# A fused attention and expert kernel on one core: slot product from PSUM, rows loaded in quarters, setup and weight work in another order

## The chip, the cores and the metric

The kernel runs on one core of a Trainium2 chip. A core has five engines that run side by side: TensorE (PE in the profile; its weight loads are PEld), VectorE (DVE), ScalarE (ACT), GpSimd (POOL) and SyncE (SP), and 16 DMA engines that move data between HBM and the on-chip memory SBUF. PSUM is the memory that TensorE writes. The metric is the device time in microseconds (us) of one execution.

## The reference, cut to what matters

```
x: 32 batches x 256 tokens x 128; 16 heads of 8; 8 experts, top 2, hidden 256
mod = silu(c) @ wmod -> shift, scale, gate for both halves (sa, ca, ga, sb, cb, gb)
h = layernorm(x) * (1 + ca) + sa
q, k, v = h @ w_qkv.T + b_qkv;  std = q.k / sqrt(8)
write_lines, read_lines = exterior products of four 4-vectors per head, each over its norm
incidence = read_lines . J(write_lines)
logits = std + incidence * decay ** (distance) * bias_scale  for the past;  causal mask
x = x + ga * (softmax(logits) @ v @ w_out.T + b_out)
h = layernorm(x) * (1 + cb) + sb
the two largest of h @ Wg take the token; out = sum of weight * (silu(h@W1) * (h@W2)) @ W3
x = x + gb * out
```

## The kernel before

It has three parts, each a block with one program per engine. Between two blocks all engines meet.

**setup** loads the weights and x, turns the projection matrices, works out the modulation `mod`, the decay table `decay` (16 heads x 128 distances per partition) and many constants. SyncE loads the projection weights, x in eight parts (L232) and then the experts' W1, W2 (L235) and W3 (L236). GpSimd makes masks and clears tiles, stores zero rows to HBM with four DMAs of its own queue (L286), and last of all cuts the decay table by an affine select (L295), after ScalarE's exponential (L345). VectorE fills the decay's arguments (L395) and only then takes the modulation and its gates (L398 to L408).

**attend** runs a pipeline written out by hand. An iteration b = -4 ... 35 has eight slots p = 0 ... 7, and each slot works for several batches at once: on batch b the scores and exponentials of heads 2p and 2p+1, on batch b+1 the prescores (a bound on the maximum of each row), on b+2 and b+3 the projections and the lines, on b-1 the output, on b-2 the second norm and the routing, on b-3 the ranks and the scatter to the experts' rows. The table JOBS says in which slot TensorE does which small job. Every engine runs its list in order and waits on semaphores.

Per slot TensorE does `scores` (L631 to L633) into the one tile sc, `incidences` (L620) and `prescores` (L644 to L646) into the one tile pre. VectorE adds tt to sc (L794), makes the next tt out of inc and decay (L827) and takes the maxima of pre (L806, and L811 after four of them). ScalarE takes the exponential (L1033). 

The keys and queries go through HBM: they are split in three bf16 parts (high, middle, low) and stored by SyncE (L554), six DMAs for the dims and twelve for the lines of a batch, and read back as rows with three DMAs per half of the heads (L579 KT 480 KB, L580 queries 336 KB, L581 QI 144 KB). TensorE waits for a half in front of its first prescores, in slots 1 and 5 of iteration b for batch b+1. In SyncE's list a half of rows follows the load of peaks (L586), which waits for ScalarE, and is followed by the next stores. GpSimd works out the low part of the lines (L1133) in slot 3, behind the outer products (L1236, four instructions) and the crosses (L1245, L1247: one and three instructions) of slot 2; in slot 4 the counts (L1208, L1210) and the first scatter follow.

Routing on VectorE, slot 3, for batch b-3: L820 adds the experts' bases to the ranks that TensorE left in PSUM (L738 to L741), L880 multiplies by the choice `hot`, L885 takes the maximum, which is the row to scatter to, and L889 to L894 work out the two weights. GpSimd scatters with four indirect DMAs (L1223).

After the last iteration ScalarE copies the experts' weights into w_hi (L1112) and VectorE, behind the table of tiles (L950 to L970), subtracts to get w_lo (L974).

**experts** runs 136 tiles of 128 rows over a ring of 16: SyncE loads a tile (L1358), TensorE turns and multiplies it (L1377 to L1402). ScalarE's first instruction is the load of the gate rows (L1439, 2 MB, first read at the very end).

## Time and profile before

| | us |
|---|---|
| median of three timed runs | 1242.65 |
| lowest, highest | 1239.29, 1244.85 |
| the profiled execution | 1247.23 |
| its span in the trace | 1245.4 |
| TensorE busy (share of the span) | 996.9 (80%) |
| VectorE busy | 909.1 (73%) |
| ScalarE busy | 716.2 (58%) |
| GpSimd busy | 815.0 (65%) |
| DMA queue of SyncE, share of 16 engines | 43.3% |

The shares are averages over three very different stages: setup up to 28.8 us, attention up to about 940, experts and the final sum after that. The rows further down come from five views. Busy time by stretch gives for a stretch of the span what each engine worked. The timeline gives instructions in order: start, duration, engine, line, operation, output and inputs, count, and in brackets the engine's idle time in front of it with what ended it. Groups by line give the count, busy time and mean of all instructions of a line within a stretch, and the idle time in front of them. Waits give who waited for whom. The DMA issues give size and time to landing.

### The profile page before, as it was taken

How to read it: one execution, taken by the hardware profiler on the slowest of the kernel's cores; microseconds unless marked ns; L12 is line 12 of the kernel's file. 1: busy time of each engine (PE TensorE's matmuls, PEld its weight loads, DVE VectorE, ACT ScalarE, POOL GpSimd, SP SyncE). 2: the span in 40 equal slices, each digit the busy share in tenths (PEclk: the TensorE clock that was granted, in tenths of full speed). 3: DMA queues.
4: the chain of work that ended last, by engine and by line, in shares of the span. 5: the costliest groups of instructions: out<-in, count | busy, mean ns of one | idle time of the engine just before them, and what ended most of it. 6: DMA issues, size and time to landing. Idle time of an engine off the chain costs nothing. (4 is left out here: it accounts for less than half of the span.)

```text
span 1245.4 us, 30939 instructions
## 1 busy us (share of the span) xinstructions
PE 996.9 (80%) x9409; PEld 783.2 (63%) x9409; DVE 909.1 (73%) x2318; ACT 716.2 (58%) x1612; POOL 815.0 (65%) x1381
## 2 busy tenths in 40 slices
PE   2348888989898989998898989887725888888767
PEld 2236667766677767776777767766524777777653
DVE  6347888878898899889988998888644454444437
ACT  3326676767767776767776777764433444444430
POOL 6676667877787878787787878773351555555440
PEclk9999999999999999999999999999956999999988
DMA  9056565565656565656656565654113222222229
GB/s 284 29 147 161 135 163 146 157 163 133 178 139 176 142 174 146 169 149 163 158 150 167 154 165 142 176 136 130 35 43 118 77 69 73 73 74 76 67 83 352
DMA packets 206097, 170.44 MB, mean 137 GB/s; under 512 B 56944, under 2 KB 183408, under 8 KB 205808
## 3 DMA queue, kind: packets, MB, share of 16 engines
q1 hardware_dynamic: 194400, 143.21, 43.3%
q0 software_dynamic: 8704, 18.04, 4.7%
q10 hardware_dynamic: 2832, 7.20, 1.5%
q8 instruction: 81, 1.33, 0.5%
q14 instruction: 80, 0.66, 0.2%
HBM read 90.81 MB, written 76.78 MB: 135 GB/s over the span
## 5 line engine op out<-in xcount | busy, mean ns | idle before, releaser
L1033 ACT ACTIVATE PT<-sc 128x768 f32<-128x768 f32 x256 | 206.7, 807 | 234.7 <-DVE sc L794 224.8
L806 DVE TENSOR_REDUCE peak<-pre 128x6 f32<-128x768 f32 x256 | 243.6, 952 | 88.4 <-PE pre L646 82.3
L1542 POOL DMA_INDIRECT yab<-y_out,xt x136 | 131.4, 966 | 143.3 <-DVE y_out L1488 106.8
L794 DVE TENSOR_TENSOR sc<-sc,tt 128x512 f32<-128x512 f32 x256 | 176.8, 691 | 17.2 <-PE sc L633 16.1
L1223 POOL DMA_INDIRECT xg<-stage,slot_i x128 | 130.6, 1020 | 76.8 <-DVE stage L894 46.0
L827 DVE TENSOR_TENSOR tt<-inc,decay 128x512 f32<-128x512 f32 x256 | 174.2, 681 | 0.3 <-PE inc L620 0.3
L631 PE MATMUL sc<-queries,KT 128*128 128x256 bf16 x512 | 142.1, 278 | 34.5 <-ACT PT L1033 24.9
L644 PE MATMUL pre<-KT,queries 120*128 120x128 bf16 x512 | 115.7, 226 | 58.3 <-DMA QI<-kq_rows 52.8
L646 PE MATMUL pre<-causal,identb 128*128 128x256 bf16 x512 | 143.2, 280 | 0.0
L645 PE MATMUL pre<-KT,queries 120*128 120x256 bf16 x512 | 141.9, 277 | 0.0
L633 PE MATMUL sc<-identb,causal 128*128 128x256 bf16 x512 | 140.7, 275 | 0.0
L1452 ACT ACTIVATE silu<-up 128x256 f32<-128x256 f32 x136 | 52.8, 388 | 127.8 <-PE up L1386 109.2
L1495 DVE TENSOR_TENSOR hid<-silu,up 128x256 f32<-128x256 f32 x136 | 57.0, 419 | 81.0 <-ACT silu L1452 51.0
L632 PE MATMUL sc<-queries,KT 128*128 128x128 bf16 x512 | 112.9, 220 | 0.0
L644 PEld LDWEIGHTS pre<-KT,queries 120*128 120x128 bf16 x512 | 50.9, 99 | 86.6 <-DMA QI<-kq_rows 62.1
L631 PEld LDWEIGHTS sc<-queries,KT 128*128 128x128 bf16 x512 | 51.0, 100 | 77.7 <-ACT PT L1033 61.7
L620 PE MATMUL inc<-QI,KT 128*128 128x128 bf16 x1024 | 99.7, 220 | 0.1
L1236 POOL TENSOR_TENSOR outer<-lines 128x256 f32<-128x256 f32 x128 | 89.1, 726 | 5.7 <-ACT lines L997 5.7
L1402 PE MATMUL y<-w,hidT 128*128 x544 | 86.9, 284 | 2.6 <-ACT hidT L1462 1.3
L660 PE MATMUL pv<-PT,VP 128*32 128x256 f32 x1024 | 84.1, 391 | 1.5 <-ACT PT L1033 1.5
L1488 DVE TENSOR_SCALAR y_out<-y,xt 128x128 f32<-128x128 f32 x136 | 47.2, 347 | 50.1 <-PE y L1402 43.6
L1394 PE MATMUL hidT_ps<-ident,hid 128*128 128x128 f32 x272 | 55.4, 287 | 32.6 <-DVE hid L1495 30.9
(263 smaller groups left out, 2824.1 us busy)
## 6 DMA issues: line engine op xcount, KB each, us to landing
KT<-kq_rows SPq DMA_DIRECT2D x64, 480.0 KB
queries<-kq_rows SPq DMA_DIRECT2D x64, 336.0 KB
kq_rows<-dim_part SPq DMA_DIRECT2D x64, 192.0 KB, 3.0
kq_rows<-line_part SPq DMA_DIRECT2D x64, 144.0 KB
QI<-kq_rows SPq DMA_DIRECT2D x64, 144.0 KB
xt<-xg SPq DMA_DIRECT2D x136, 65.0 KB
kq_rows<-dim_part SPq DMA_DIRECT2D x64, 128.0 KB, 2.8
kq_rows<-line_part SPq DMA_DIRECT2D x64, 96.0 KB
```

Source lines behind the costliest of these rows:

```text
L631: nc.tensor.matmul(sc[:, n, 0:T], KT[par][:, h, 0:P], QF[par][:, h, :], start=True, stop=False)
L632: nc.tensor.matmul(sc[:, n, T:3 * P], KT[par][:, h, P:T], QF[par][:, h, P:T], start=False, stop=False)
L633: last = nc.tensor.matmul(diagonal(sc, n), causal[:], identb[:].unsqueeze(1).broadcast_to([P, 2, P]), start=False, stop=True)
L644: nc.tensor.matmul(pre[:, n, 0:P], QF[par][0:TOP, h, 0:P], KT[par][0:TOP, h, 0:P], start=True, stop=False)
L645: nc.tensor.matmul(pre[:, n, P:3 * P], QF[par][0:TOP, h, P:T], KT[par][0:TOP, h, :], start=False, stop=False)
L646: last = nc.tensor.matmul(diagonal(pre, n), identb[:], causal[:].unsqueeze(1).broadcast_to([P, 2, P]), start=False, stop=True)
L794: nc.vector.tensor_tensor(diag, diag, tt[p % 2][:], ALU.add).then_inc(added.sem, 1)
L806: nc.vector.reduce_max(peak[half][:, i:i + 2, 0:3], pre[:, :, 0:3 * P].rearrange("p n (g k) -> p n g k", g=3), AX.X)\
L827: nc.vector.tensor_tensor(tt[p % 2][:], inc[:], decay[:, 2 * p:2 * p + 2, :].unsqueeze(2).broadcast_to([P, 2, NT, P]), ALU.mult).then_inc( ...
L1033: nc.scalar.activation(PT[p % 4][:], sc[:, :, 0:3 * P], ACT.Exp).then_inc(exped.sem, 1)
L1223: nc.gpsimd.indirect_dma_start(xg[0:E * CAP, :], bass.IndirectOffsetOnAxis(slot_i[:, t, k:k + 1], 0), stage[par][:, t, k, :], None).then_i ...
L1542: nc.gpsimd.indirect_dma_start(yab, bass.IndirectOffsetOnAxis(xt[r][:, D:D + 1].bitcast(i32), 0), y_out[r % 8][:], None).then_inc(y_sent[r ...
```

## The change

What it does, in the order of the diff:

(In the diff a long run of removed lines, and unchanged lines, are cut to "...", and eight columns of indentation are left out.)

- setup: the loads of W1, W2 and W3 go from SyncE's setup list to the head of its attention list. The four DMAs of zero rows go from GpSimd to ScalarE, which waits for their landing at the end of setup. TensorE's modulation products go ahead of the bias columns, VectorE's modulation and gates ahead of the decay's arguments, and the store of the gate rows ahead of the decay's exponential. The decay's mask goes into attention, to GpSimd's slot 7 of iteration -4; VectorE waits for it before its first use.
- rows: each half is loaded as two quarters of four heads, six DMAs where there were three, with a semaphore per quarter, and TensorE waits in every second slot.
- rank: TensorE adds the experts' bases itself with a product of the identity and `ebase`; VectorE then needs one product from PSUM, in place of a sum from PSUM and a product in SBUF.
- GpSimd: the crosses are parted from the outer products and go behind the lines' low part.
- the experts' weights: a copy per slot on ScalarE in iteration 32, a subtraction per slot on VectorE in iteration 33.
- experts: the load of the gate rows goes to tile 16.

```diff
@@ -230,10 +231,6 @@
             sp.dma_start(v["x_all"][:, n * k * D:(n + 1) * k * D].rearrange("p (n d) -> p n d", d=D), xd[:, n * k:(n + 1) * k, :]).then_inc(ld_x, 16)
-        w_raw = v["w_lo"][:].bitcast(fp32).rearrange("p e (n h) -> p e n h", n=2)
-        for n, w in enumerate(("W1", "W2")):
-            sp.dma_start(w_raw[:, :, n, :], v[w].rearrange("e p h -> p e h")).then_inc(v["w_loaded"], 16)
-        sp.dma_start(v["w3"][:], v["W3"].rearrange("e (m p) d -> p e m d", p=P)).then_inc(v["w_loaded"], 16)
         sp.wait_ge(ld_x, 128)
@@ -279,22 +276,13 @@
         step(nc.gpsimd.tensor_copy(v["identb"][:], ident[:]))
-        step(nc.gpsimd.memset(zero_rows[:], 0.0))
-        for par in range(2):
...
+        nc.gpsimd.memset(zero_rows[:], 0.0).then_inc(zeros_ok, 1)
         ones_pair = 0x3F803F80
...
             step(nc.gpsimd.memset(v["VP"][m][:, :, :, DH:DH + 1], 1.0))
-        pool.wait_ge(exp_ok, 1)
-        nc.gpsimd.affine_select(out=decay[:], in_=decay[:], compare_op=ALU.is_gt, fill=0.0, base=0,
-                                pattern=[[0, H], [1, P]], channel_multiplier=-1).then_inc(setup_done, 1)
-        pool.wait_ge(setup_done, 1)
@@ -308,21 +296,21 @@
         last.then_inc(wT_ok, 1)
+        pe.wait_ge(silu_ok, 1)
+        for m in range(6):
+            last = nc.tensor.matmul(tC[:, m * NB:(m + 1) * NB], wmod_sb[:, m * D:(m + 1) * D], silu_c[:],
+                                    start=True, stop=True)
+        last.then_inc(mod_ok, 1)
         pe.wait_ge(az_ok, 2)
...
                          start=True, stop=True).then_inc(columns_ok, 1)
+        pe.wait_ge(gates_ok, 1)
+        nc.tensor.transpose(tA[0:NB, 0:D], mod[:, 5, :], ident[:]).then_inc(rows_ok, 1)
         pe.wait_ge(columns_ok, 2)
         nc.tensor.matmul(tD[:, 4:5], v["w_outT"][:], bias_v[:], start=True, stop=True).then_inc(out_bias_ok, 1)
-        pe.wait_ge(silu_ok, 1)
-        for m in range(6):
...
@@ -340,15 +328,23 @@
         nc.scalar.activation(lz[:], ez[:], ACT.Ln, bias=1.0).then_inc(ln_ok, 1)
-        act.wait_ge(arg_ok, 1)
-        nc.scalar.activation(v["line_decay"][:], v["line_decay"][:], ACT.Exp, scale=line_log[:]).then_inc(act_step, 1)
-        nc.scalar.activation(decay[:], decay[:], ACT.Exp).then_inc(exp_ok, 1)
+        act.wait_ge(zeros_ok, 1)
+        for par in range(2):
+            for kq, half in ((0, 1), (1, 0)):
+                main = v["kq_rows"][par][kq, 0:RAW0].rearrange("(s r) h t -> r h s t", s=NS)[DH:NM]
+                act.dma_start(main.rearrange("r h s t -> (r h) s t")[:, :, half * P:half * P + P],
+                              zero_rows[0:6 * H].unsqueeze(1).broadcast_to([6 * H, NS, P])).then_inc(v["zeros_stored"], 16)
         act.wait_ge(ld_v, 64)
         act.wait_ge(rows_ok, 1)
-        nc.scalar.activation(v["modr"][:], tA[0:NB, 0:D], ACT.Copy)\
-          .then_inc(act_step, 1)
-        act.wait_ge(act_step, 3)
+        nc.scalar.activation(v["modr"][:], tA[0:NB, 0:D], ACT.Copy).then_inc(act_step, 1)
+        act.wait_ge(act_step, 2)
         act.dma_start(v["mod_rows"], v["modr"][:]).then_inc(v["mod_stored"], 16)
+        act.wait_ge(columns_ok, 2)
+        nc.scalar.activation(v["line_decay"][:], v["line_decay"][:], ACT.Exp, scale=line_log[:])
+        act.wait_ge(arg_ok, 1)
+        nc.scalar.activation(decay[:], decay[:], ACT.Exp).then_inc(exp_ok, 1)
+        act.wait_ge(exp_ok, 1)
+        act.wait_ge(v["zeros_stored"], 16 * 4)
@@ -383,29 +379,29 @@
         nc.vector.tensor_copy(log_rep[:], ez[:].unsqueeze(1).broadcast_to([P, 6, H])).then_inc(az_ok, 1)
+        dve.wait_ge(mod_ok, 1)
+        step(nc.vector.tensor_copy(mod[:], tC[:, 0:6 * NB].rearrange("p (m b) -> p m b", b=NB)))
+        for m in (1, 4):
+            nc.vector.tensor_scalar(mod[:, m, :], mod[:, m, :], 1.0, None, ALU.add)
+        gates = mod[:, 2:6:3, :]
+
+        nc.vector.tensor_scalar(ga_sign[:], gates, 0.0, 2.0, ALU.is_ge, ALU.mult)
+        step(nc.vector.tensor_scalar(ga_two[:], gates, -1.0, None, ALU.mult))
+        step(nc.vector.tensor_tensor(ga_abs[:], ga_two[:], gates, ALU.max))
+        step(nc.vector.tensor_scalar(ga_two[:], ga_abs[:], 0.25, None, ALU.max))
+        step(nc.vector.tensor_scalar(ga_abs[:], ga_sign[:], 1.0, None, ALU.subtract))
+        nc.vector.tensor_tensor(gates, ga_abs[:], ga_two[:], ALU.mult).then_inc(gates_ok, 1)
         dve.wait_ge(cols_ok, 1)
...
         nc.vector.tensor_copy(bias_v[:], tD[:, 2:3]).then_inc(columns_ok, 1)
-        dve.wait_ge(out_bias_ok, 1)
-        step(nc.vector.tensor_tensor(bias_out[:], tD[:, 4:5], bout[:], ALU.add))
         for h in range(H):
...
         last.then_inc(arg_ok, 1)
-        dve.wait_ge(mod_ok, 1)
-        step(nc.vector.tensor_copy(mod[:], tC[:, 0:6 * NB].rearrange("p (m b) -> p m b", b=NB)))
...
+        dve.wait_ge(out_bias_ok, 1)
+        step(nc.vector.tensor_tensor(bias_out[:], tD[:, 4:5], bout[:], ALU.add))
         dve.wait_ge(gates_ok, 1)
@@ -458,7 +454,7 @@
 hot = a("hot", [P, NT, 2, E]); hot_sum = a("hot_sum", [P, NT, E], bf16)
-slot_at = a("slot_at", [P, NT, E]); slot_pick = a("slot_pick", [P, NT, 2, E])
+slot_pick = a("slot_pick", [P, NT, 2, E])
 slot_i = a("slot_i", [P, NT, 2], i32)
@@ -493,7 +489,7 @@
 dims_stored, lines_stored = signal("dims_stored", 16 * 6), signal("lines_stored", 16 * 12)
-rows_loaded = [signal(f"rows_loaded{n}", 48) for n in range(2)]
+rows_loaded = [signal(f"rows_loaded{n}", 48) for n in range(4)]
 pre_ready, maxed = signal("pre_ready", 8), signal("maxed", 8)
@@ -502,9 +498,10 @@
 recip = signal("recip", 2)
-route_step = signal("route_step", 6)
+route_step = signal("route_step", 5)
 gap_exp, probs, hot_added, slots_ready, run_added = (
     signal(n) for n in ("gap_exp", "probs", "hot_added", "slots_ready", "run_added"))
+decay_cut = sem("decay_cut")
 numbered, run_half = signal("numbered"), signal("run_half")
@@ -569,16 +566,17 @@
-            heads = slice(8 * half, 8 * half + 8)
             hold(dims_stored, jb)
...
             hold(pre_ready, jb - 1, 4 * half + 1)
-            done = rows_loaded[half].sem
-            sp.dma_start(KT[par][0:TOP, heads, :], kq_rows[par][0, :, heads, :]).then_inc(done, 16)
-            sp.dma_start(QF[par][0:RAW0, heads, :], kq_rows[par][1, 0:RAW0, heads, :]).then_inc(done, 16)
-            sp.dma_start(QI[par][RAW0:TOP, heads, :], kq_rows[par][1, RAW0:TOP, heads, :]).then_inc(done, 16)
+            for quarter in (2 * half, 2 * half + 1):
+                heads = slice(4 * quarter, 4 * quarter + 4)
+                done = rows_loaded[quarter].sem
+                sp.dma_start(KT[par][0:TOP, heads, :], kq_rows[par][0, :, heads, :]).then_inc(done, 16)
+                sp.dma_start(QF[par][0:RAW0, heads, :], kq_rows[par][1, 0:RAW0, heads, :]).then_inc(done, 16)
+                sp.dma_start(QI[par][RAW0:TOP, heads, :], kq_rows[par][1, RAW0:TOP, heads, :]).then_inc(done, 16)
@@ -599,6 +597,10 @@
+        w_raw = v["w_lo"][:].bitcast(fp32).rearrange("p e (n h) -> p e n h", n=2)
+        for n, w in enumerate(("W1", "W2")):
+            sp.dma_start(w_raw[:, :, n, :], v[w].rearrange("e p h -> p e h")).then_inc(v["w_loaded"], 16)
+        sp.dma_start(v["w3"][:], v["W3"].rearrange("e (m p) d -> p e m d", p=P)).then_inc(v["w_loaded"], 16)
         sp.wait_ge(v["mod_stored"], 16)
@@ -636,8 +638,8 @@
-            if p % 4 == 0:
-                wait(pe, rows_loaded[p // 4], b)
+            if p % 2 == 0:
+                wait(pe, rows_loaded[p // 2], b)
             wait(pe, maxed, b, p)
@@ -738,6 +740,8 @@
                 nc.tensor.matmul(B[:, E:2 * E], onesb[:], hot_sum[:, 0, :], start=False, stop=False)
+                nc.tensor.matmul(B[:, 0:NT * E].rearrange("p (t e) -> p t e", t=NT), ident[:],
+                                 v["ebase"][:].unsqueeze(1).broadcast_to([P, NT, E]), start=False, stop=False)
                 last = nc.tensor.matmul(B[:, 0:NT * E].rearrange("p (t e) -> p t e", t=NT), onesb[:],
@@ -810,18 +814,29 @@
                 extras(b, par, p)
+                if b == NB + 1:
+                    weights_rest(p)
+
+        def weights_rest(e):
+
+            dve.wait_ge(w_high, e + 1)
+            nc.vector.tensor_tensor(w_lo[:, e, :], w_lo[:, e, :].bitcast(fp32), w_hi[:, e, :].bitcast(fp32), ALU.subtract)
...
                 wait(dve, ready["rank"], jb)
+                wait(dve, slots_ready, jb - 1)
                 B = bank[BANK["rank"]]
-                nc.vector.tensor_tensor(slot_at[:], B[:, 0:NT * E].rearrange("p (t e) -> p t e", t=NT),
-                                        v["ebase"][:].unsqueeze(1).broadcast_to([P, NT, E]), ALU.add)\
-                  .then_inc(used["rank"].sem, 1)
+                nc.vector.tensor_tensor(
+                    slot_pick[:], hot[:], B[:, 0:NT * E].rearrange("p (t e) -> p t e", t=NT).unsqueeze(2)
+                    .broadcast_to([P, NT, 2, E]), ALU.mult).then_inc(used["rank"].sem, 1)
+
         def weigh(b, p):
+            if (b, p) == (0, 0):
+                dve.wait_ge(decay_cut, 1)
             wait(dve, inc_ready, b, p + 1)
@@ -877,19 +892,15 @@
                 wait(dve, used["rank"], jb)
-                nc.vector.tensor_tensor(slot_pick[:], hot[:],
-                                        slot_at[:].unsqueeze(2).broadcast_to([P, NT, 2, E]), ALU.mult)\
-                  .then_inc(route_step.sem, 1)
-                wait(dve, route_step, jb, 4)
                 wait(dve, scattered, jb - 1)
...
                 nc.vector.tensor_scalar(eg1[:], egap[:], 1.0, None, ALU.add).then_inc(route_step.sem, 1)
+                wait(dve, route_step, jb, 4)
+                nc.vector.reciprocal(mine[:, :, 0, D + 1], eg1[:]).then_inc(route_step.sem, 1)
                 wait(dve, route_step, jb, 5)
-                nc.vector.reciprocal(mine[:, :, 0, D + 1], eg1[:]).then_inc(route_step.sem, 1)
-                wait(dve, route_step, jb, 6)
                 for t in range(NT):
@@ -969,9 +980,6 @@
                                        op0=ALU.mult, op1=ALU.add)
-        for e in range(E):
-            dve.wait_ge(w_high, e + 1)
-            nc.vector.tensor_tensor(w_lo[:, e, :], w_lo[:, e, :].bitcast(fp32), w_hi[:, e, :].bitcast(fp32), ALU.subtract)
@@ -1092,6 +1100,16 @@
                     normalise(b + 4, rs1[:, b + 4], nb1[:, b + 4], xhat, ready["norm"], normed)
+                if b == NB:
+                    weights_first(p)
+
+        def weights_first(e):
+
+            if e == 0:
+                act.wait_ge(v["w_loaded"], 16 * 3)
+                wait(act, sc_ready, NB - 1)
+                wait(act, pre_ready, NB - 1)
+            nc.scalar.activation(w_hi[:, e, :], w_lo[:, e, :].bitcast(fp32), ACT.Copy).then_inc(w_high, 1)
@@ -1105,11 +1123,6 @@
         iterations(act, body)
-        act.wait_ge(v["w_loaded"], 16 * 3)
-        wait(act, sc_ready, NB - 1)
...
         act.wait_ge(pads_known, 1)
@@ -1127,10 +1140,12 @@
                 if p == 2 and live(b + 3):
-                    crosses(b + 3)
+                    outer_products(b + 3)
                 if p == 3 and live(b + 2):
...
                     nc.gpsimd.tensor_tensor(line_part[:, 2, :], line_rest[:], line_part[:, 1, :], ALU.subtract).then_inc(line_low.sem, 1)
+                if p == 3 and live(b + 3):
+                    crosses(b + 3)
                 if p == 4 and live(b - 3):
@@ -1149,6 +1164,9 @@
                     first_inverse(b + 4)
+                if (b, p) == (-4, 7):
+                    nc.gpsimd.affine_select(out=decay[:], in_=decay[:], compare_op=ALU.is_gt, fill=0.0, base=0,
+                                            pattern=[[0, H], [1, P]], channel_multiplier=-1).then_inc(decay_cut, 1)
                 if p == 7 and live(b - 2):
@@ -1224,7 +1242,7 @@
-        def crosses(jb):
+        def outer_products(jb):
@@ -1238,6 +1256,9 @@
             last.then_inc(outered.sem, 1)
+
+        def crosses(jb):
+
             wait(pool, outered, jb)
@@ -1436,8 +1457,6 @@
     def _(act):
-        act.dma_start(gate_row[:].rearrange("p b d -> p (b d)"),
-                      v["mod_rows"].unsqueeze(0).broadcast_to([P, NB, D])).then_inc(gates_loaded, 16)
         nc.scalar.preload_act_table(ACT.Silu)
@@ -1454,6 +1473,9 @@
                     keep_h(i, r - 1)
+                if (i, r) == (1, 0):
+                    act.dma_start(gate_row[:].rearrange("p b d -> p (b d)"),
+                                  v["mod_rows"].unsqueeze(0).broadcast_to([P, NB, D])).then_inc(gates_loaded, 16)
```

## Rows read from the trace of the kernel before

**Rows 1.** By stretch: us, PE, PEld, DVE, ACT, POOL busy; clock, DMA share, GB/s

```profile
170.70:829.40 658.70, 588.97 (x6482) 463.33 (x6479) 581.50 (x1353) 471.37 (x960) 526.39 (x963) 1.00 0.59 157
```

**Rows 2.** Timeline, ScalarE: first exponentials of periods 3 and 29

```profile
170.70 0.81 ACT L1033 ACTIVATE PT<-sc 128x768 f32<-128x768 f32 x1
...
829.40 0.81 ACT L1033 ACTIVATE PT<-sc 128x768 f32<-128x768 f32 x1 [0.85 <-DVE sc L794]
```

**Rows 3.** Timeline, VectorE and GpSimd, 553 to 564 us

```profile
553.04 0.17 DVE L811 TENSOR_REDUCE peak<-peak 128x8 f32<-128x16 f32 x1
...
557.83 2.80 POOL L1236 TENSOR_TENSOR outer<-lines 128x256 f32<-128x256 f32 x4
...
562.10 1.65 POOL L1133 TENSOR_TENSOR line_part<-line_rest,line_part 96x768 bf16<-96x768 f32 x1
...
562.38 1.40 DVE L889 TENSOR_SCALAR eg<-egap 128x2 f32<-128x2 f32 x1
```

**Rows 4.** Timeline, TensorE and VectorE, 416 to 418 us

```profile
416.57 0.23 PE L644 MATMUL pre<-KT,queries 120*128 120x128 bf16 x1 [1.59 <-DMA QI<-kq_rows]
...
417.34 0.96 DVE L806 TENSOR_REDUCE peak<-pre 128x6 f32<-128x768 f32 x1 [0.70 <-issue]
```

**Rows 5.** Groups by line, 170.7 to 829.4 us: busy, mean ns | idle before

```profile
L880 DVE TENSOR_TENSOR slot_pick<-hot,slot_at 128x32 f32<-128x32 f32 x26 | 18.9, 728 | 0.0
L889 DVE TENSOR_SCALAR eg<-egap 128x2 f32<-128x2 f32 x26 | 18.0, 692 | 0.0
...
L644 PE MATMUL pre<-KT,queries 120*128 120x128 bf16 x418 | 93.2, 223 | 32.4 <-DMA QI<-kq_rows 32.3
...
L746 PE MATMUL bank<-wg_sb,h2T 128*128 128x8 f32 x104 | 13.6, 239 | 0.0
```

**Rows 6.** Timeline, SyncE's queue and TensorE, 549 to 556 us, and the stretch

```profile
549.16 0.36 SPq L581 DMA_DIRECT2D QI<-kq_rows  x1
552.09 3.05 SPq L554 DMA_DIRECT2D kq_rows<-dim_part  x6
...
555.43 0.23 PE L644 MATMUL pre<-KT,queries 120*128 120x128 bf16 x1 [0.39 <-DMA QI<-kq_rows]
...
549.50:553.00 3.50, 3.50 (x45) 2.79 (x45) 3.33 (x8) 3.29 (x7) 2.97 (x4) 1.00 0.87 231
```

**Rows 7.** Timeline, end of setup, and SyncE's wait for x

```profile
21.45 1.56 SPq L236 DMA_DIRECT2D w<-in_L_ffn_W  x1
...
25.32 2.00 POOL L295 TENSOR_SCALAR_AFFINE_SELECT decay<-decay 128x2048 f32<-128x2048 f32 x1 [3.76 <-ACT decay L345]
28.83 0.06 DVE L937 MEMSET three_halves<- 128x1 f32 x1 [3.97 <-PEq L126]
...
SPq L223 <- DMA x_all<-in_L_attn_x: 0.2, 1, 0.2
```

**Rows 8.** Timeline, TensorE, the first prescores

```profile
78.15 0.29 PE L644 MATMUL pre<-KT,queries 120*128 120x128 bf16 x1 [4.51 <-DMA QI<-kq_rows]
```

**Rows 9.** Groups by line, VectorE: 96.7 to 170.7 us, then 829.4 to 903.4

```profile
L806 DVE TENSOR_REDUCE peak<-pre 128x6 f32<-128x768 f32 x24 | 22.9, 953 | 10.0 <-PE pre L646 10.0
...
L806 DVE TENSOR_REDUCE peak<-pre 128x6 f32<-128x768 f32 x17 | 16.2, 952 | 7.9 <-PE pre L646 5.3 <-issue 2.5
```

**Rows 10.** Timeline, end of attention and first tile; then two DMA issues

```profile
931.69 0.96 POOL L1223 DMA_INDIRECT xg<-stage,slot_i  x1 [0.30 <-issue]
...
934.05 4.89 DVE L974 TENSOR_TENSOR w_lo<-w_lo,queries 128x512 fp32r<-128x512 f32 x8
...
940.76 9.08 SPq L1358 DMA_DIRECT2D xt<-xg  x11
948.12 0.69 PE L1377 MATMUL xT<-ident,xt 128*128 128x128 f32 x2 [23.02 <-DMA xt<-xg]
...
kq_rows<-dim_part SPq DMA_DIRECT2D x64, 64.0 KB, 2.9
gate_row<-mod_rows ACTq DMA_DIRECT2D x1, 2048.0 KB, 7.6
```

33 lines of the change are left out of this document (11 added, 22 removed).

## Prediction

> **What bounds the kernel now.** I read the busy times by stretch first, then cut the span into its stages with the timeline. The attention loop is most of it: from the first exponential of period 3 to that of period 29 (26 periods, one batch each) it takes 829.40 - 170.70 = 658.7 us, 25.33 us a period [rows 2], and in it TensorE is busy 589.0 us and VectorE 581.5, close to 90% each, with GpSimd at 80% and the 16 DMA engines at 0.59 [rows 1]. Two engines at 90% feed each other through single PSUM tiles, so what costs time is whatever makes one of them stand still. The groups by line name two such things.
>
> The first is on VectorE and looks like work. Two tiny instructions on 128x32 and 128x2 elements, L880 and L889, have means of 728 and 692 ns; their undisturbed times are about 0.18 and 0.16. Over 26 periods that is 18.9 + 18.0 - 26 x 0.34 = 28 us too much [rows 5]. In one period L889 starts at 562.38, GpSimd's L1133 (the low part of the lines) has been running since 562.10, and L889 ends at 563.78, 0.03 after L1133 does [rows 3]. Either L880 or L889 is caught so in nearly all later periods, for some 1.2 to 1.5 us.
>
> The second is TensorE's wait for the loaded rows, 32.3 us at L644 over the 26 periods [rows 5]. In the same kind of period it is only 0.39 us [rows 6]; in a period where neither tiny instruction is caught it is 1.59, and VectorE stands idle 0.70 after it [rows 4]. So the two causes cover each other: taking away only the first lets the second grow.
>
> Outside the loop: 28.8 us of setup, 68 us in which the first batches are prepared, and a tail in which VectorE still works on the weights until 938.94 and the experts' first matmul starts at 948.12 [rows 7, 8, 10].
>
> **The change part by part.** The sum is made against the profiled execution (1247.23 us, span 1245.4), 4.6 above the median of the three timed runs, 1242.65; I take the savings off the median.
>
> *Slot product and crosses in the loop.* L820 and L880 become one product that reads PSUM, and on GpSimd the line's low part (L1133) goes ahead of the crosses, right behind the outer products. In the period of [rows 3] GpSimd's order is fixed from the moment L811 starts (553.04): the outer products end at 560.63, 7.6 later, with hardly a pause. L1133 would then end at 560.63 + 1.65 = 562.28, not at 563.75. VectorE's L889 comes about 0.3 earlier without the old L880 and L820 (0.18 + 0.1), near 562.1, and 0.4 earlier again where the wait for rows goes. It is then still caught, but only to 562.3: its end moves from 563.78 to 562.3, 1.45 us. Bounds: 0 if it is caught as before by something else, 1.7 where L880 was the one caught. The crosses end when they ended before, so their readers lose nothing.
>
> The Trainium skill, "SBUF — State Buffer", section "Who interferes with whom", says that VectorE and GpSimd share a port pair, that the one that starts first holds it for its whole instruction, and that this touches VectorE instructions in a two-port mode or with two SBUF inputs. By that rule the new product (one SBUF input) goes free, while L889 stays exposed; the ends in [rows 3] agree. What it would make of the time is a rival below.
>
> *Rank.* TensorE gets an fp32 product of the identity with the expert bases. The nearest is L746, four instructions of 239 ns for two products that overlap by half, so about 0.25 us; bounds 0.05 (hidden under a wait) and 0.5 [rows 5]. It lies before the scores of slot 3 and would push VectorE by some 0.2, in the stretch that GpSimd now fixes at 562.3. I take 0.
>
> *Rows in quarters.* While a half is being moved the DMA engines deliver 231 GB/s [rows 6]; a half is 960 KB and takes about 4.2 of the 6.3 us between the issue of its last part (549.16) and L644 (555.43), so the first quarter, half the bytes, lands about 2.1 us earlier. Bounds: 0 (a transfer's cost is all latency) to 2.5. That covers 0.39 and 1.59. VectorE then gains the 0.70 of an uncaught period and the 0.4 of slot 1. Three more issues of 0.36 us stand in SyncE's queue per half, in front of the next stores: rows end their issue at 549.52, the next stores start at 552.09 because they wait for GpSimd [rows 6]. 1.1 fits in 2.6 and costs nothing; without that gap it costs 1.1 per half.
>
> The Trainium skill, "DMA: Bandwidth & Descriptors", section "Measured", speaks against quarters: it wants 1 MiB per DMA and puts 2.0 us of fixed cost on each. By the row the DMAs of one queue overlap (three of them, 231 GB/s), so I take the row; by the rule six in a row would cost 6 us more and the waits would stay.
>
> For the 26 periods: the 28 us of excess are some 20 catches at about 1.4. Where L889 was caught the period falls by 1.45, where L880 was, by 1.7 (half of them each, 31.5 us), and the 6 uncaught ones by 0.7 (4). 36 us, 1.4 a period, to 23.9; bounds 18 and 52. In the first three periods VectorE idles 10.0 us before L806; about 1.1 of it per period is TensorE's own work, and of the rest I take 4. After 829.4 it idles 7.9 there with two batches to load; I take 4.5 [rows 9].
>
> *Start.* x_all lands at about 23.2 (SyncE ends its last issue at 23.0 and waits 0.2 for it), but setup ends with the decay's mask, 25.32 + 2.00, and VectorE starts the next block at 28.83, 1.5 later [rows 7]. With the mask moved behind the first inverse (GpSimd then waits for the first lines, and the mask's first reader is period 0), the zero rows off GpSimd and the modulation in front of the decay, x is what ends last: 23.2 + 1.5 = 24.7, 4 us. The zero rows and the decay's exponential may come close to it: bounds 2 and 4.5. The three loads of weights, issued by SyncE at the head of the next block, take some 5 us of its queue and 3 MB of transfer, while the first batch is only being normalised and its first store is a whole batch's preparation away: 0. ScalarE's four DMA issues lie in its wait for VectorE.
>
> Then the first rows: TensorE waits 4.51 us at 78.15 for them [rows 8]. The line's low part comes 1.45 earlier and the quarter 2.1, together 3.5; I take 3, bounds 0 and 4.5.
>
> *Tail and experts.* The copies and subtractions of the weights (4.89 us on VectorE) move into slots where both engines mostly wait. VectorE's tables then end at 934.05; GpSimd's last scatter ends its issue at 932.65 and lands, at 2.9 for a small transfer, by 935.5 [rows 10]. So 3.4 to 4.9 is given back, and a copy of 0.6 between the last norms can cost that much; I take 4, bounds 3 and 5. The gate rows (2048 KB, 7.6 us) leave the start: the first tile was issued at 940.76 and used at 948.12, 7.4 later, where small transfers land in about 2.9 [rows 10]. 4.5, bounds 2 and 5. At tile 16 the gate rows run beside loads issued a ring ahead: 0, or the same 4.5 if the ring were empty.
>
> **Sum:** 36 + 4 + 4.5 + 4 + 3 + 4 + 4.5 = 60, so 1247 - 60 = 1187 for the profiled execution, and 1242.65 - 60 = 1183 for the median.
>
> **The rivals.**
> *The rows wait takes the place of the block.* If quarters do not land earlier, L644 in every period waits the 1.6 of [rows 4] or more and VectorE idles 0.7: the loop gives 18 instead of 36, first and last periods nothing, the first rows 1.5 instead of 3. 1183 + 18 + 8.5 + 1.5 = 1211. Against it: a half's bytes take most of its time. Chance 0.16.
> *The block moves on* (the skill's rule, above). If L889 arrives after the line's low part and under the crosses, whose four instructions are about 1.47 us together, it is held by one of them for up to 0.6: 26 x 0.6 = 16, 1199. For it: the arrival is within 0.3 us of the change-over. Chance 0.13.
> *Nothing else holds.* TensorE and VectorE close up further, to about 23.1 a period, TensorE's 22.6 plus half a microsecond: 26 x 0.6 = 16 more, 1167. Chance 0.13.
> *Slower: SyncE's queue becomes the chain.* 6 issues x 0.36 = 2.2 us a period, 69 in 32, if rows and stores had no gap between them; the loop's other gains would be lost behind it and only setup, tail and experts (12.5) stay: 1242.65 + 69 - 12.5 = 1299. It decides from the point where the gap of 2.6 us falls under 1.1. Chance 0.03.
> *It does little:* the loop is held by a latency that none of these rows names, and the moved work is hidden as it was. 1240, 0.02.
>
> **How the numbers follow.** Forecast 1183 with chance 0.53 (1173 to 1196). Range 1166 to 1211: it takes in the faster case and most of the two slower-than-forecast ones. A measurement of this kernel tells about 0.5% from no change: faster 0.95, same 0.02, slower 0.03.
>
> **What would show it.** L889 and the new product: mean under 0.4 us, with L889 ending with the line's low part. L644's wait for DMA under 5 us in all. Period 23.5 to 24.1 us. VectorE's first instruction of attention near 24.7; tables near the last scatter's landing, first expert matmul 3 us after its issue. Wrong: L644 still waits over 1 us in most periods, or another VectorE instruction grows by 1 us, or GpSimd's order lets split peaks come late.

## The result, and the profile of the changed kernel

| | before | changed |
|---|---|---|
| median, us | 1242.35 | 1174.92 |
| lowest, highest | 1239.29, 1244.85 | 1172.63, 1178.69 |
| profiled execution, its span | 1247.23, 1245.4 | 1177.21, 1175.5 |

The medians are of four executions each, the profiled ones among them. The ratio is 0.9461, with a 95% interval of 0.9424 to 0.9499: 67.4 us less, where 60 were forecast. The stages of the two profiled executions, cut at the same instructions:

| stage (where it ends) | before | changed | gain | forecast |
|---|---|---|---|---|
| setup (VectorE's first instruction of attention) | 28.8 | 24.6 | 4.2 | 4 |
| first batches (first exponential) | 67.9 | 66.6 | 1.3 | 3 |
| periods 0 to 2 | 74.0 | 68.3 | 5.7 | 4 |
| the loop, periods 3 to 28 | 658.7 | 616.7 | 42.0 | 36 |
| periods 29 to 31 (last exponential) | 70.9 | 63.2 | 7.7 | 4.5 |
| tail (issue of the first tile) | 40.4 | 39.7 | 0.7 | 4 |
| first tile (its first matmul) | 7.4 | 1.8 | 5.5 | 4.5 |
| experts and final sum | 297.3 | 294.5 | 2.7 | 0 |

The last row's 2.7 us is no gain that can be told from chance: in the experiments below on the chips of the first two sessions, this stage takes 289.7 to 294.7 us with the changed kernel's code and 291.4 and 296.0 with that of before.

The loop first, which is here the 26 periods 3 to 28. The stretch that answers to [rows 1], and three groups that answer to [rows 5] (L646 is the old L644, L900 the old L889, called eg from here on, and L832 the new product in the place of L820 and L880, the slot product):

```profile
159.50:776.20 616.70, 585.74 (x6528) 466.51 (x6527) 562.71 (x1326) 472.51 (x960) 525.22 (x963) 1.00 0.58 168
```

```profile
L646 PE MATMUL pre<-KT,queries 120*128 120x128 bf16 x417 | 92.5, 222 | 0.7 <-issue 0.7
L900 DVE TENSOR_SCALAR eg<-egap 128x2 f32<-128x2 f32 x26 | 17.5, 672 | 0.0
L832 DVE TENSOR_TENSOR slot_pick<-hot,bank 128x32 f32<-128x32 f32 x26 | 4.6, 177 | 0.0
```

A period is 23.72 us. TensorE's 32.3 us of waiting for rows are gone. The slot product is at its undisturbed 0.18. But the eg instruction is still at 672 ns, hardly below its 692 of before. One period of the timeline, to be read beside [rows 3]:

```profile
564.69 0.17 DVE L815 TENSOR_REDUCE peak<-peak 128x8 f32<-128x16 f32 x1
...
569.48 2.79 POOL L1254 TENSOR_TENSOR outer<-lines 128x256 f32<-128x256 f32 x4
...
572.23 1.64 POOL L1146 TENSOR_TENSOR line_part<-line_rest,line_part 96x768 bf16<-96x768 f32 x1
...
573.21 0.68 DVE L900 TENSOR_SCALAR eg<-egap 128x2 f32<-128x2 f32 x1
```

Counted from the start of the small peak reduction (L815, the old L811), the low part of the lines runs from 7.54 to 9.18 and eg ends at 9.20. Eg ends between 9.20 and 9.23 in 24 of the 26 periods, and at 9.51 in the two others. That is what was forecast (7.6 + 1.65). It looks like a confirmation; the experiments show that it is not where the gain came from.

SyncE's queue in the same period, the peaks, the last part of the second quarter and the line stores behind it:

```profile
570.37 0.73 SPq L584 DMA_DIRECT2D queries<-peakT  x1
...
573.57 0.37 SPq L579 DMA_DIRECT2D QI<-kq_rows  x1
574.06 2.12 SPq L551 DMA_DIRECT2D kq_rows<-line_part  x3
```

Setup, first rows and tail:

```profile
21.61 1.91 ACT L345 ACTIVATE decay<-decay 128x2048 f32<-128x2048 f32 x1 [0.42 <-DVE decay L401]
...
24.59 0.06 DVE L948 MEMSET three_halves<- 128x1 f32 x1 [2.67 <-PEq L126]
...
82.73 0.55 DVE L888 TENSOR_REDUCE norm_sq<-square 128x64 f32<-128x384 f32 x1 [1.34 <-ACT square L1035]
...
872.90 0.97 POOL L1241 DMA_INDIRECT xg<-stage,slot_i  x1 [0.30 <-issue]
...
879.12 2.02 SPq L1379 DMA_DIRECT2D xt<-xg  x3
880.95 0.48 PE L1398 MATMUL xT<-ident,xt 128*128 128x128 f32 x1 [14.66 <-DMA xt<-xg]
```

### The profile page after: what moved, and what is told of

It is laid out like the page before. It is cut to its first block and busy times, and to the rows that moved or that the text cites. A ratio compares the mean times of both kernels' runs of the same rounds, so it can differ in the third digit from the quotient of the medians.

```text
span 1175.5 us, 31325 instructions
## 1 busy us (share of the span) xinstructions
PE 992.1 (84%) x9473; PEld 785.6 (67%) x9473; DVE 888.5 (76%) x2286; ACT 717.9 (61%) x1612; POOL 812.0 (69%) x1377
## 3 DMA queue, kind: packets, MB, share of 16 engines
q8 instruction: 82, 1.34, 0.5%
## 5 line engine op out<-in xcount | busy, mean ns | idle before, releaser
L810 DVE TENSOR_REDUCE peak<-pre 128x6 f32<-128x768 f32 x256 | 243.5, 951 | 47.1 <-PE pre L648 46.2
L798 DVE TENSOR_TENSOR sc<-sc,tt 128x512 f32<-128x512 f32 x256 | 177.0, 691 | 18.6 <-PE sc L635 17.8
L646 PE MATMUL pre<-KT,queries 120*128 120x128 bf16 x512 | 114.8, 224 | 8.6 <-DVE peak L810 7.2
L622 PEld LDWEIGHTS inc<-QI,KT 128*128 128x128 bf16 x1024 | 79.0, 98 | 3.1 <-DVE tt L842 0.2
```

The costliest lines, as they stand in the source:

```text
L622: last = nc.tensor.matmul(inc[:, n, t, :], KT[par][:, h, blk], QI[par][:, h, blk], start=True, stop=True)
L798: nc.vector.tensor_tensor(diag, diag, tt[p % 2][:], ALU.add).then_inc(added.sem, 1)
L810: nc.vector.reduce_max(peak[half][:, i:i + 2, 0:3], pre[:, :, 0:3 * P].rearrange("p n (g k) -> p n g k", g=3), AX.X)\
```

## The experiments

Twelve kernels, in three sessions. The kernel before had medians of 1243.5, 1241.6 and 1193.7 us in them: the last four, marked "other chip", ran on a chip that is faster in the experts' stage (last section), so across sessions only ratios and loop times are compared. A ratio has an interval of 0.2 to 0.5% on either side. A loop time is that of one profiled execution: changed, gate_start, w_end and setup_old have the same code in the loop and take 616.7 to 618.3 us, so differences of up to 1.6 us are not told from chance.

| kernel | median, us | ratio to before | loop, us (26 periods) |
|---|---|---|---|
| changed | 1174.9 | 0.946 | 616.7 |
| q_only: before + quarters | 1188.8 | 0.956 | 614.2 |
| route_only: before + product and order | 1265.2 | 1.016 | 686.5 |
| halves: changed, halves again | 1251.5 | 1.006 | 674.3 |
| old_order: changed, crosses first again | 1173.2 | 0.944 | 612.8 |
| act_probs: changed, weights of routing on ScalarE | 1163.7 | 0.934 | 606.2 |
| w_end: changed, experts' weights last again | 1176.5 | 0.946 | 618.3 |
| gate_start: changed, gate rows first again | 1183.3 | 0.952 | 616.8 |
| setup_old: changed, old setup | 1182.0 | 0.950 | 618.3 |
| late (other chip): old_order + 0.7 us on VectorE | 1140.1 | 0.953 | 643.8 |
| halves_fill (other chip): halves + work for TensorE | 1191.7 | 0.998 | 672.1 |
| act_old_order (other chip): act_probs, crosses first | 1117.0 | 0.936 | 610.5 |
| lean (other chip): act_probs + bf16 bases | 1110.8 | 0.931 | 604.6 |

### One part of the loop's change at a time

q_only is the kernel before with this edit (and four semaphores instead of two):

```
-heads = slice(8 * half, 8 * half + 8)
+for quarter in (2 * half, 2 * half + 1):
+    heads = slice(4 * quarter, 4 * quarter + 4)
     sp.dma_start(KT ...); sp.dma_start(QF ...); sp.dma_start(QI ...)
-if p % 4 == 0: wait(pe, rows_loaded[p // 4], b)
+if p % 2 == 0: wait(pe, rows_loaded[p // 2], b)
```

> The kernel before with one part of the change: the rows are loaded in quarters. Theory (the two causes cover each other, and GpSimd's low part holds VectorE until 10.7 to 11.0 us after the small peak reduction of slot 0 whatever TensorE does): the wait for rows falls from 32 us in the loop to under 8, VectorE only arrives earlier at the same block, so the two tiny instructions stretch by more (28 us of excess grow to 32 or more) and the period falls by no more than 0.3 us: 1242 less 8 in the loop and 6 around it, about 1228. Rival (TensorE is the bound, so every wait of its own counts): the 32 us come back whole, about 1205. Second rival (a quarter's cost is latency, not bytes): the wait stays, 1242.

Measured: 0.9561 (0.9535 to 0.9587), the loop 44.5 us shorter, more than the whole change. The stretch and the groups:

```profile
164.10:778.30 614.20, 579.94 (x6477) 462.49 (x6476) 558.07 (x1353) 473.02 (x961) 526.35 (x963) 1.00 0.58 168
```

```profile
L645 PE MATMUL pre<-KT,queries 120*128 120x128 bf16 x417 | 92.5, 222 | 0.6 <-DMA QI<-kq_rows 0.6
...
L881 DVE TENSOR_TENSOR slot_pick<-hot,slot_at 128x32 f32<-128x32 f32 x26 | 6.2, 237 | 0.0
L890 DVE TENSOR_SCALAR eg<-egap 128x2 f32<-128x2 f32 x26 | 5.4, 207 | 0.0
```

The wait for rows is gone, and so is nearly all the stretching of both tiny instructions (728 and 692 ns in [rows 5]), though nothing on GpSimd or VectorE was changed. The timeline shows why, in a usual period and in the only bad one:

```profile
498.20 0.17 DVE L812 TENSOR_REDUCE peak<-peak 128x8 f32<-128x16 f32 x1
506.69 0.16 DVE L890 TENSOR_SCALAR eg<-egap 128x2 f32<-128x2 f32 x1
507.27 1.64 POOL L1134 TENSOR_TENSOR line_part<-line_rest,line_part 96x768 bf16<-96x768 f32 x1
...
331.11 0.17 DVE L812 TENSOR_REDUCE peak<-peak 128x8 f32<-128x16 f32 x1
333.45 0.23 PE L645 MATMUL pre<-KT,queries 120*128 120x128 bf16 x1 [0.63 <-DMA QI<-kq_rows]
340.15 1.64 POOL L1134 TENSOR_TENSOR line_part<-line_rest,line_part 96x768 bf16<-96x768 f32 x1
340.40 1.42 DVE L890 TENSOR_SCALAR eg<-egap 128x2 f32<-128x2 f32 x1
```

The low part starts 9.07 us after the small reduction in the first period and 9.04 in the second. In the first, eg arrives at 8.49 and is through. In the second TensorE had waited 0.63 for rows in slot 1, eg arrives at 9.29, 0.25 too late, and is held to 10.7. That is the usual case of before ([rows 3]: 562.38 - 553.04 = 9.34, with 0.39 us of waiting in slot 1 in [rows 6]). The trace of before says the same over all 26 periods: in 22 of them TensorE waits for rows in slot 1, by 0.19 to 1.41 us, and eg or the slot product is stretched in each; in the other four it does not wait there, and neither is stretched by more than 0.1. So the block was a consequence of the wait for rows in slot 1. My theory had the two causes side by side; the block and this wait are one. The wait in slot 5, for the second half, is the one that stands beside them.

route_only is the other part alone (the product from PSUM with the bases from TensorE, and on GpSimd outer products, low part, crosses):

```
-crosses(b + 3)                       # slot 2
+outer_products(b + 3)
 nc.gpsimd.tensor_tensor(line_part[:, 2, :], line_rest[:], ...)   # slot 3
+crosses(b + 3)
```

> The kernel before with the other part of the change in the loop: slot product from PSUM, the bases added by TensorE, and the line's low part ahead of the crosses; rows still in halves. Theory: the block on VectorE ends 9.2 us after the small peak reduction instead of 10.7; since the low part also reaches HBM 1.45 earlier, the rows come earlier by the same, and their wait grows only from 32 to about 35 us. The period falls from 25.33 by 1.1 to 24.2: 1242 less 29 in the loop and 4 around it, about 1209. Rival (the waits for rows take the place of the block): they grow to 1.6 us a period, 42 us or more, and the period stays above 24.7: 1225.

Measured: 1.0165 (1.0125 to 1.0204), 1.6% slower and clear of the noise. The rival has the growth of the waits (42 us or more, measured 52.8); that the kernel gets slower, neither theory said.

```profile
171.40:857.90 686.50, 607.80 (x6536) 486.72 (x6533) 561.79 (x1327) 470.45 (x960) 526.69 (x963) 0.96 0.57 151
```

```profile
L644 PE MATMUL pre<-KT,queries 120*128 120x128 bf16 x418 | 95.6, 229 | 53.2 <-DMA QI<-kq_rows 52.8 <-DVE peak L808 0.2
```

The block is shorter and the wait for rows goes from 32.3 to 52.8. The two slots go opposite ways: in slot 1 it falls from 11.3 us in 22 periods to 4.2 in 9, in slot 5 it grows from 21.0 to 48.6. First route_only, then before, from the last issue of a half to the matmul that waited for it:

```profile
549.47 0.36 SPq L581 DMA_DIRECT2D QI<-kq_rows  x1
...
555.68 0.23 PE L644 MATMUL pre<-KT,queries 120*128 120x128 bf16 x1 [1.78 <-DMA QI<-kq_rows]
```

```profile
561.40 0.36 SPq L581 DMA_DIRECT2D QI<-kq_rows  x1
...
567.40 0.23 PE L644 MATMUL pre<-KT,queries 120*128 120x128 bf16 x1 [0.60 <-DMA QI<-kq_rows]
```

5.85 and 5.64 us after the end of the issue, and 15.46 and 15.81 us after the first exponential of their periods (540.22 and 551.59). The second half's rows land at that point whether VectorE is blocked or not; the block of 1.4 us in slot 3 lay inside this wait, and blocked and free periods of before differ by 0.6 to 0.9 us in length, with the wait in slot 1 included. That the low part comes 1.45 earlier does not help this half: SyncE issues it behind the load of the peaks and ahead of the stores of that low part, which concerns the next batch. It does help the first half, which SyncE issues behind those stores.

That explains why there is next to no gain; it does not explain a loss. Of the 26 periods 7 take 24.2 to 24.6 us and 14 over 27. In a long one (616.5 to 643.5, rows awaited until 632.24), where the number after POOL's (1.00, 0.72) is the granted clock:

```profile
616.50:631.50 15.00, 13.41 (x145) 10.56 (x142) 13.24 (x30) 12.21 (x26) 12.73 (x26) 1.00 0.67 183
631.50:637.50 6.00, 5.26 (x49) 4.53 (x50) 3.89 (x8) 2.84 (x7) 5.19 (x10) 0.72 0.46 118
```

After the wait of 1.92 us TensorE gets 0.72 of its clock for some 6 us: part of them at the lower level, 1.2 GHz. Eg is also held beyond 9.2: in eight of the periods it arrives later, at 9.1 to 9.5, is held by one of the crosses, which now stand behind the low part, and ends at 9.76 to 9.78.

halves is the changed kernel with whole halves again (the edit of q_only, reversed).

> The changed kernel with one part undone: the rows are loaded in halves again. Theory: TensorE waits 0.4 to 1.6 us for rows in slots 1 and 5, VectorE idles 0.4 to 0.7 for it, period 24.2 instead of 23.72, and the first rows come 2 us later: 1175 plus 13 plus 5, about 1193. Rival (VectorE is then the bound and hides TensorE's wait): 1177 to 1180.

Measured: 1.0062 (1.0036 to 1.0088), 77 us above the changed kernel and worse than both theories; TensorE waits 54.3 us for rows in the loop, and 14 of the 26 periods take 26 to 28 us. Quarters are worth 55 us to the old kernel and 77 to the changed one (by the loop alone 44.5 and 57.6).

halves_fill asks whether the clock makes the long periods: halves, with this ahead of the wait of slot 5:

```
+if p == 4:
+    for _ in range(16):
+        nc.tensor.matmul(diagonal(pre, 0), identb[:], causal ..., start=True, stop=True)
 if p % 4 == 0: wait(pe, rows_loaded[p // 4], b)
```

> The changed kernel with rows in halves (1251.5; periods of 24.2 and of 26 to 28 us mixed, granted clock 0.94 in the long ones, 1.00 in the short), and TensorE does 16 products of 128x256 bf16 (1.8 us at full clock, results unused) where it otherwise waits 1.2 to 2.4 us for the second half's rows in slot 5. Theory (the long periods are the clock's answer to that wait): the clock stays at 1.00, nearly all periods are 24.2 to 24.6, and the time falls by about 20 periods times 1.6, 32 us, to 1220. Rival (the long periods come from late rows and from VectorE and GpSimd running behind them): they stay, and the time is 1250 or more.

Measured: 0.9980 (0.9959 to 1.0001) against 1.0062 for halves, in the loop 672.1 against 674.3. By its total the theory falls. Its mechanism holds. The end of the filled wait, and the next period's start:

```profile
233.06 0.23 PE L649 MATMUL pre<-KT,queries 120*128 120x128 bf16 x1 [0.51 <-DMA QI<-kq_rows]
...
242.00 0.81 ACT L1044 ACTIVATE PT<-sc 128x768 f32<-128x768 f32 x1
```

242.00 - 233.06 = 8.94 us from the rows to the next period, and 8.94 or 8.95 in all 19 periods where the trace shows the wait. In route_only the same distance is 9.0 to 9.1 in the short periods and 11.0 to 11.8 in those over 27. So the long periods owe 2 to 2.7 us to the clock that falls behind the wait, and with TensorE kept busy it stays up (1.00 in this period). What eats the gain is the first part: the rows now land 16.4 to 18.0 us into the period instead of 15.2 to 16.8. Part of that is a later issue: SyncE starts on the second half 9.5 us into the period (median; 8.8 in halves), and this goes with a wait in slot 1, where TensorE now stands in all 26 periods, 23.9 us in total, against 14 periods and 6.4 us in halves. What made the first half late in turn is open, and it was not tried with fewer products.

### The order on GpSimd, and arrival

old_order is the changed kernel with the crosses ahead of the low part:

```
 outer_products(b + 3)                 # slot 2
+crosses(b + 3)
 nc.gpsimd.tensor_tensor(line_part[:, 2, :], line_rest[:], ...)   # slot 3
-crosses(b + 3)
```

> The changed kernel with one part undone: on GpSimd the crosses stand ahead of the line's low part again. In the changed kernel VectorE's eg instruction arrives 8.5 us after the small peak reduction, the low part holds it from 7.53 to 9.2. With the old order the crosses (four short instructions, together 1.5) run from 7.5 to 9.0 and the low part from 9.0 to 10.7. Theory (a block lasts as long as the one GpSimd instruction that runs on arrival): eg is held by one cross for 0.1 to 0.5 and ends by 8.9, the low part comes 1.45 later and the rows with it, which the quarters still cover for most of the half: 1170 to 1180. Rival (the order is what bought the loop's gain): VectorE slips behind the crosses, is caught by the low part until 10.7 and stays there, period 25.0 or more: 1208.

Measured: 0.9444 (0.9412 to 0.9475), no different from the changed kernel; in the loop 612.8 against 616.7. Usual periods are 23.38, and one, with 0.87 us of waiting for rows, 25.55. The theory holds: beside quarters the order bought nothing. It put the low part where eg arrives (8.4 to 8.7) and holds it to 9.2 each time, 0.3 us a period; with the old order it is held by a cross for 0.16 at most and ends by 8.85 in all but one of the periods.

late asks whether it is a question of arrival. It adds to old_order:

```
+for n in range(4):
+    nc.vector.reduce_max(later[:, n, :], slot_pick ..., AX.X)    # 128x32, unused
 nc.vector.reduce_max(slot_i ..., AX.X)
```

> The changed kernel with the old order on GpSimd (1173.2), and VectorE does four more reductions of 128x32 elements (0.18 us each, results unused) ahead of the slot's maximum and of eg in slot 3. There eg arrived 8.36 to 8.54 us after the small peak reduction, and GpSimd's low part starts 9.04 after it. Theory (the block is a question of arrival, a gate at 9.04): eg now arrives at 9.1 to 9.3, is held by the low part until 10.7, so 0.7 us of work costs 2.1 a period: 25.3 to 25.6 instead of 23.45, and 1173 plus 55, about 1228. Rival (work costs its own time): 0.7 a period at most, period 24.1, 1173 plus 20, 1193 or less.

Measured: 0.9527 (0.9486 to 0.9568), against 0.9444 for old_order. By the medians the added work costs about 10 us, which is the rival's size (20 or less) and not the theory's 55. The profiled execution, at 1154.5 us, is the slowest of the four; the others took 1130.3, 1137.6 and 1142.5. Two of its periods, a blocked and a free one:

```profile
557.64 0.17 DVE L816 TENSOR_REDUCE peak<-peak 128x8 f32<-128x16 f32 x1
566.69 1.64 POOL L1150 TENSOR_TENSOR line_part<-line_rest,line_part 96x768 bf16<-96x768 f32 x1
566.70 1.66 DVE L903 TENSOR_SCALAR eg<-egap 128x2 f32<-128x2 f32 x1
...
582.71 0.17 DVE L816 TENSOR_REDUCE peak<-peak 128x8 f32<-128x16 f32 x1
591.75 1.68 POOL L1150 TENSOR_TENSOR line_part<-line_rest,line_part 96x768 bf16<-96x768 f32 x1
591.76 0.16 DVE L903 TENSOR_SCALAR eg<-egap 128x2 f32<-128x2 f32 x1
```

In both eg comes at 9.05, the instant in which the crosses end and the low part starts. When GpSimd goes first, 20 times in 26, the period is 25.06 to 25.09; otherwise 23.6 to 23.9. So 0.7 us more work costs 0.25 of itself, and 1.44 more when the block follows. That is the theory's step, but at a tie and not as a certainty: it makes the profiled loop 31 us longer, not 55. An execution with no blocked period would take some 1135 us (an estimate: old_order's ratio on this chip, 1127, and 32 times 0.25). The three others lie near that, so by this estimate they had few blocked periods or none; no trace shows how many.

### What is left in the changed loop

act_probs takes eg, the reciprocal and the two products from VectorE:

```
-nc.vector.tensor_scalar(eg1[:], egap[:], 1.0, ...); nc.vector.reciprocal(...); 2 x nc.vector.tensor_scalar(...)
+nc.scalar.activation(eg1[:], egap[:], ACT.Ln, bias=1.0)                       # slot 1
+nc.scalar.activation(mine[:, :, 0, D + 1], eg1[:], ACT.Exp, scale=-1.0)
+nc.scalar.activation(mine[:, :, 1, D + 1], mine[:, :, 0, D + 1], ACT.Identity, scale=-1.0, bias=1.0)
```

> The changed kernel, and the two routing weights leave VectorE: ScalarE takes exp of the gap, ln(1 + it), exp of the negative and one minus that, three small instructions more, in slot 1, where it idles 2.0 us; VectorE loses eg, the reciprocal and two products, 0.66 us undisturbed and about 1.2 with the block of 0.53. What this tells: in the changed kernel GpSimd's low part (7.53 to 9.2 us after the small peak reduction) holds eg in every period until 9.2. Theory (this standing block is all that its loop has over the 23.4 of the undisturbed periods with the old order): period 23.2 to 23.4, 8 to 13 us less in the loop, about 1164. Rival (TensorE with 22.6 us of work a period and 1.2 idle is the bound): nothing changes, 1173 to 1177. Rival on the other side (three more instructions on ScalarE push the line copies of slot 1 and with them GpSimd): 1180 or more.

Measured: 0.9344 (0.9296 to 0.9392), 1163.7. The period is 23.23 to 23.25 in 19 of 26; the theory holds. (The instructions on ScalarE also moved from slot 2 to slot 1, so this is not the block alone.) VectorE is busy 537.1 us in the loop against 562.7, ScalarE 492.9 against 472.5, and the stretch is 606.20:

```profile
159.70:765.90 606.20, 579.26 (x6529) 468.97 (x6527) 537.12 (x1223) 492.94 (x1039) 526.44 (x963) 1.00 0.58 170
```

act_old_order and lean try the two last pieces. The first reverses the order on GpSimd, as old_order does.

> The kernel with the routing weights on ScalarE (1163.7), and GpSimd's crosses ahead of the line's low part again. No instruction of VectorE stands open to the block now. Theory (the new order only shifts the crosses 1.6 us back, and VectorE waits 0.38 us a period for the squares in slot 4 behind them): the old order gives this wait back and the first rows 1.4 us, and the rows, 1.6 later, still land in time: period 23.2 to 23.3, 1158 to 1163. Rival (the earlier low part covers rows that would be late): period 23.6 or more and single ones of 25, 1170.

Measured: 0.9359 (0.9337 to 0.9382), by the ratio no different from act_probs. The profiled loop is 4.3 us longer, not shorter, and 10 of 26 periods are 23.6 to 24.0. The first batches gained 0.2, not 1.4. VectorE's wait of 0.38 in slot 4 is still there. The path of the loss is SyncE's queue. TensorE waits for the load of peaks in front of the next batch's first scores, in 13 periods and 8.7 us in total, for 0.5 us in act_probs. The worst of them, with SyncE's rows:

```profile
407.63 7.47 SPq L552 DMA_DIRECT2D kq_rows<-line_part  x12
415.22 0.75 SPq L585 DMA_DIRECT2D queries<-peakT  x1
417.56 0.27 PE L634 MATMUL sc<-queries,KT 128*128 128x256 bf16 x1 [1.25 <-DMA queries<-peakT]
```

The load of peaks stands behind the twelve line stores, and these behind the low part. With the old order the low part and the stores come later, and in 14 of 26 periods the load follows the last store by only 0.12 us, so it had been waiting for its turn in the queue (in act_probs in one period, with 1.6 us between them as a median). Once nothing on VectorE can be blocked, the earlier low part is therefore worth having; by how much, two traces from different chips tell only roughly. In old_order the same wait takes 5.2 us, and in q_only 4.1.

lean exchanges the product of the bases (128 e in 64 rows and 2 e in the others add up to an expert's base):

```
-nc.tensor.matmul(B ..., ident[:], v["ebase"] ...)    # fp32
+nc.tensor.matmul(B ..., onesb[:], v["ebase"] ...)    # bf16, columns add up to the bases
```

> The kernel with the routing weights on ScalarE (1163.7), and the experts' bases as one bf16 product: a matrix whose columns add up to them (128 e in 64 rows, 2 e in the others), turned by the matrix of ones, instead of the fp32 product with the identity, which is two instructions, 0.38 us on TensorE and a wait of 0.32 on VectorE for the scores behind it. Theory (TensorE, idle 0.9 to 1.0 of 23.24 us, is what a period waits for): 0.2 a period, 1163.7 less 6, 1158. Rival (VectorE hides it): 1162 to 1165.

Measured: 0.9307 (0.9285 to 0.9328); period 23.20 against 23.24, 1.6 us in the loop. The rival is nearer: the wait of 0.32 on VectorE went, and another, in slot 1, grew by 0.15. These 1.6 us alone are not told from chance. It is the fastest version here, with 82.9 us less than before in its session, and its interval lies below the changed kernel's.

### Outside the loop

Each undoes one part in the changed kernel. setup_old takes back the whole setup: the decay's arguments ahead of the modulation, the zero rows in GpSimd's queue, the loads of the weights behind x, and

```
-if (b, p) == (-4, 7): nc.gpsimd.affine_select(out=decay[:], ...)   # attention
+pool.wait_ge(exp_ok, 1); nc.gpsimd.affine_select(out=decay[:], ...)   # end of setup
```

> The changed kernel with the setup of before: decay ahead of modulation, zero rows from GpSimd's queue, the decay's mask and the weights' loads in setup. Theory: VectorE's first instruction of attention moves from 24.6 to 28.8, and since the order of the rest stays, everything behind it by the same 4.2: 1179. Rival (the three loads of weights at the head of SyncE's attention list and the mask on GpSimd in iteration -4 cost the first rows something, which comes back here): 1176 to 1177. Rival on the other side (setup's loads compete with x): 1182.

Measured 1182.0, 7 us more. VectorE's first instruction is at 28.95, 4.4 later, as by the theory; the loop is 1.6 longer and every other stage within 2.3 us of the changed kernel's, which is about what two executions of it differ by. The median is that of the rival on the other side (1182), but its reason, loads that compete with x in setup, could only show in setup's own 4.4 us; the profiled spans differ by 4.9.

```
-if b == NB: weights_first(p)          # ScalarE, a copy a slot
-if b == NB + 1: weights_rest(p)       # VectorE, a subtraction a slot
+for e in range(E): ...                # both behind the last iteration
```

> The changed kernel with one part undone: the copies and subtractions of the experts' weights stand behind the last iteration and behind the table of tiles again. Theory from the trace of the changed kernel: there the barrier waits for the last scatter's landing, 3.4 us after its issue, and the last iterations are 2.1 us longer than before; undone, the last scatter comes 2 us earlier, VectorE ends 4.9 later than its table, so the barrier moves by no more than +1: 1174 to 1177. Rival (what was predicted: 4 us of the change come from here): 1179.

Measured 1176.5. VectorE's subtractions end at 880.17, and the first tile is issued at 882.02, which is 1.6 us later, counted from the start of period 29, than in the changed kernel (104.45 against 102.88). The theory holds; 4 had been forecast.

```profile
875.29 4.88 DVE L978 TENSOR_TENSOR w_lo<-w_lo,queries 128x512 fp32r<-128x512 f32 x8
...
882.02 16.87 SPq L1370 DMA_DIRECT2D xt<-xg  x19
```

```
+act.dma_start(gate_row ...)           # ahead of the activation table
-if (i, r) == (1, 0): act.dma_start(gate_row ...)
```

> The changed kernel with one part undone: the 2 MB of gate rows are loaded at the head of the experts' block again. Theory: they stand in the DMA engines ahead of the first tile, which then takes 7.4 instead of 1.8 us from its issue to the first matmul: 1175 plus 5.5, 1180. Rival (the first tile was late because of the scattered rows' landing, which now ends earlier): 1175.

Measured 1183.3. The gate rows' issue, the first tile's and its first matmul, 7.46 us apart, against 1.83:

```profile
878.18 0.34 ACTq L1460 DMA_DIRECT2D gate_row<-mod_rows  x1
...
878.63 21.51 SPq L1379 DMA_DIRECT2D xt<-xg  x19
...
886.09 0.69 PE L1398 MATMUL xT<-ident,xt 128*128 128x128 f32 x2 [20.37 <-DMA xt<-xg]
```

5.6 us by the trace, 8.4 by the medians, where the theory has 5.5. The theory holds; what the other 3 us are is open.

## Why the prediction was right, and where it was not

The total was right, at 1175 for 1183 in a range of 1166 to 1211. The loop's 36 us (42.0 measured) were near as a sum and wrong in their parts: one term was far too large and another far too small, and that they made up for each other was luck.

*Slot product and crosses* was given 31.5 of the 36 us ("where L889 was caught the period falls by 1.45"). This step failed. By itself it makes the kernel 1.6% slower, since it lengthens a wait behind which TensorE's clock falls; on top of quarters, the product and the bases bring 1.4 us (614.2 to 612.8, not told from chance) and the order costs 4.0 (612.8 to 616.7). The reading of the block was sound: it ends with the low part, and its new end at 9.2 came as worked out. What failed is the inference that time lost inside an instruction is time lost by the period. Before, the second half's rows landed 15.2 to 16.1 us into the period in 22 of 26, blocked or not. The evidence was in the rows chosen: the period around [rows 4], with no block, waits 1.59 us for rows, all of it in slot 5; the period of [rows 3], blocked for 1.4, waits 0.39 in slot 1 and 0.60 in slot 5, and the two differ by 0.6 us in length. The prediction set the 0.39 of slot 1 beside the 1.59 of slot 5, as if they were the same wait. The prediction said that the two cover each other and then added both gains.

*Rank* was taken as 0. The fp32 product is two instructions of 263 ns a period on TensorE, and VectorE waits 0.32 us for the scores behind it; lean takes both away and the loop falls by 1.6 us, so 0 was near enough.

*Rows in quarters* had the mechanism right (bytes, not latency: waits of up to 1.76 us vanish, so the first quarter lands about that much earlier or more, against 2.1 worked out) and the size wrong. It was given the 4 us of VectorE's idle time in six periods, and is worth 44.5. Missing was that without the wait in slot 1 VectorE reaches eg before the low part starts, so that 25 of the 28 us of blocks go with it, and that of the 1.6 us of TensorE's wait in slot 5 about 1.1 count: the unblocked periods fall from 24.5 to 23.4, the blocked from 25.1 to 25.4 to the same, and three of 26.6 to 27.9 go altogether. The rule of the Trainium skill, "DMA: Bandwidth & Descriptors", section "Measured" (batch DMAs to 1 MiB and more), that was set aside there would have given no gain; DMAs of 72 to 240 KB, six in a row, gave 44.5. (The 2.0 us of fixed cost that the prediction puts under that heading stand on the same page in its section "Anatomy of one DMA — SWDGE (gpsimd) path"; both are for DMAs that GpSimd issues, and these are SyncE's.)

*The port.* The product with an input from PSUM takes 0.18 us in every period of the kernels that have it, and eg is held when one of these GpSimd instructions runs as it arrives. The traces so agree with the Trainium skill, "SBUF — State Buffer", section "Who interferes with whom". The rival built on it ("the block moves on", held by a cross for up to 0.6) is not what the changed kernel does; old_order shows it at 0.16 us a period at most, and route_only at 0.1 to 0.5 in eight periods.

*SyncE's queue*: six loads take 3.6 us with the peaks (570.37 to 573.94) and the stores follow 0.12 later, so the gap of 2.1 to 2.6 is used up, but no queue behind it is late in the changed kernel. The slower rival stayed away. It was nearer than it seems: with the low part late (q_only, old_order, act_old_order) TensorE waits 4.1 to 8.7 us in the loop for the load of peaks in this queue.

*Setup* was right to 0.1: the decay's exponential ends at 23.52, and x lands at about 23.0 (SyncE's last issue of it ends at 17.8 and it waits 5.2), so the exponential, named as coming close, is the last by half a microsecond.

*First rows*: the first prescores start 3.1 us earlier within attention (46.2 for 49.3 us after its start), as forecast, but 1.8 of it is given back before the first exponential. VectorE waits 1.34 us at 82.73 for the squares, which hang on the crosses, now a slot later, so "their readers lose nothing" does not hold here. It is not the cause of the loss, though: old_order does not have this wait and gains 0.15 us by it, since TensorE then waits 1.16 for the load of peaks at 89.02. From the first prescores to the first exponential all kernels but the one before take 20.1 to 20.9 us, that one 18.5; why is open.

*First and last periods* were 1.7 and 3.2 more than forecast, from the same under-sized quarters: q_only alone has 5.2 and 5.5.

*Tail*: 4 was forecast from VectorE's 4.89 us, 0.7 came by the stages, and w_end gives the moved weights 1.6, of which 0.8 lie in the last periods. Two things were missed. With the weights in the slots the last scatter starts 33.5 us after the last exponential's start, for 31.3 both before and in w_end: 2.1 us are lost there (in act_probs, with the weights in the slots but less work on VectorE, it is 31.5). And VectorE's table ends at 875.32, but the first tile is issued only at 879.12. In w_end that issue comes 1.8 behind VectorE's end; 1.8 taken off leaves 877.3, which is 3.4 us after the end of the last scatter's issue (872.90 + 0.97). The scatter's landing is the likely end of the stage; the trace does not name it. *Experts' start* was 5.5 for 4.5, right.

## What to carry to other kernels

A stretched instruction is worth its excess only if nothing later in the same period waits for an event at a fixed time; lay the two kinds of period side by side before adding their gains. When a stall comes in just those periods that also have another one earlier, remove the earlier (here the transfer), since the other can be its echo: an engine that arrives 0.3 us late meets a block of 1.4. And a transfer that gates an engine in one piece should be cut so that the first consumer needs only the first piece.

## What the runs showed of the hardware beyond that

In route_only TensorE's waits in slot 5, of 1.60 to 2.46 us, are followed in 16 periods by 6 us with a mean granted clock of 0.72 or less, and in ten, after waits of 1.47 to 2.01, by a clock of 1.00. The wait's length alone does not decide: a wait of 1.72 stands in a period of 27.0 and in one of 24.5. Products that nobody reads kept the clock at 1.00 behind all 19 waits of halves_fill.

Chips differ by stage. The same experts' code, from the first to the last tile's first matmul, takes 198 to 199 us on the chip of the last four runs and 243 to 249 on the others, with the same instructions. The stretch in lean, and then in act_probs:

```profile
864.30:1063.60 199.30, 198.98 (x1326) 173.71 (x1326) 117.31 (x399) 110.82 (x400) 125.72 (x130) 0.98 0.36 100
```

```profile
868.00:1114.00 246.00, 213.07 (x1325) 176.41 (x1326) 121.61 (x399) 113.88 (x400) 125.39 (x130) 0.97 0.30 81
```

The instructions take the same times on both (in the loop 0.81 us for an exponential, here 0.39 for a silu). On the slower chips ScalarE stands idle between the end of TensorE's last product for a tile and its own silu: 56 us over the 136 tiles of act_probs, where a silu starts up to 4.4 us late, and 5 us in lean, where it is 0.04 each time. That is about the size of the difference; what holds ScalarE the trace does not name, so this stays open.
